# A graph network on one core: the sort's second layer as exact bfloat16 products, one group later, and shorter stretches between the stages

## The chip, the core and the metric

One core of a Trainium2 chip runs the whole program in one launch. The metric is the device time of that launch in microseconds; the time before is the median of three runs, 7716.12 us (7713.63 to 7728.18). Below, PE is the matrix engine (TensorE), DVE is VectorE, ACT is ScalarE, POOL is GpSimd and SP the engine that queues most DMAs.

## The reference, cut to what matters

The input is a table x of 6250 nodes x 64 features and 200,000 edges (src, dst, 24 attributes, a weight). Four graph layers follow each other, each with a residual and a layer norm:

```python
x = _layernorm(x + L0(x, edge_attr_8, edge_attr_16, edge_weight, ..., src, dst))
x = _layernorm(x + L1(x, edge_index, edge_weight))   # 3 proximal smoothing steps
x = _layernorm(x + L2(x, edge_index, W1, b1, W2, b2)) # polynomial of degree 5
x = _layernorm(x + L3(x, edge_index, W1, b1, W2, b2)) # two graph convolutions
# in L0, for each edge, with two small perceptrons over its attributes:
_mlp2 = lambda x, W1, b1, W2, b2: silu(x @ W1 + b1) @ W2 + b2
# their two results are added, weighted by the edge's cutoff and used in the message
# in L3:
h = x @ W; agg = segment_sum(h[src] * (dinv[src]*dinv[dst])[:, None], dst)
return agg + h * (1.0 / deg)[:, None] + b
```

The two perceptrons of an edge are computed as one: 24 attributes to 128 hidden values (8 to 64 and 16 to 64), a silu, and 128 to 64. All of this is float32 in the reference.

## The kernel before

The nodes are held as 50 blocks (`NB`) of 125 lanes (`NL`), so that a table of all nodes is 125 x 3200 float32. The stages run one after the other, each in a block of its own, with every engine meeting at its end: `front` (q, k, v projections), `sort_edges`, `build_graph`, `spill_messages`, a layer norm, three calls of `scale_of_degree`, `smooth`, a layer norm, the polynomial, a layer norm, `project` and `convolve` twice, and the last layer norm.

**The sort.** `sort_edges` writes each edge's row of 70 float32 to a place in DRAM given by its two node blocks and its rank there. It goes through 196 groups (`NG`) of 8 tiles (`G`) of 128 edges (`ST`); buffers with a number 0 or 1 change with the group. For one group:

- PE: two float32 products 24 x 512 give the hidden values (L403, named `ps_h`). Then, for each of the 8 tiles, one product reads the running count of edges per block pair (L410, `ps_r`) and one adds the tile to that count (L414, `ps_c`); ACT copies the new count from PSUM (L382) before the next L410 may run. From the fifth tile on, each tile is followed by two tiles of the second layer (L424, `ps_m`, float32, `hidden` as the stationary operand and `w2` as the moving one). In the second tile stand two small products (L431, L433, `ps_f`) that number the edges of the group before which found their place full; they wait for DVE's `flagged`.
- ACT: the silu of both hidden halves (L379) and the eight count copies.
- DVE: `group_hots` of a group (L455 to L464: the one-hot rows `hot_d`, `hot_s` over 50 blocks for its edges, and `hot_dt`, the same one-hot transposed, 50 x 1024 bfloat16), then `places` of the group before it (L483 to L511): eight comparisons of keys, the rank, the message rows (`biased` = second layer + bias at L497, times the weight at L499, the other six columns at L500), then, behind a wait for L433, the row number `row_at` of each edge (L502 to L511). Most of these are linked, that is, each waits for the one before by a semaphore.
- POOL: eight indirect stores (L351) of 128 rows each, started by `rows_ready`, which L511 counts up.
- SP: loads the attributes and keys two groups ahead.

**Between the stages.** `spill_messages` (L994 to L1074) handles the edges that found no place: 125 at a time, it loads rows, gathers q and k, v by index, sums the messages of equal targets with a product and adds them to DRAM; here it runs twice. It starts by setting a 125 x 3366 buffer to zero on POOL and writing it out. `smooth` starts with five passes of DVE over the whole table (L1782 to L1786): scale x, split it in three bfloat16 parts whose sum is exact. `posted` is then counted up for all 25 pairs of blocks at once, and PE starts. The polynomial and the convolutions start the same way (L2045, `to_parts` L1162 to L1165). Before each convolution `project` multiplies all 50 blocks by a 64 x 64 matrix, with PE, ACT and DVE taking two blocks at a time (L561 to L587).

## Time and profile before

| | |
|---|---|
| median of three runs | 7716.12 us |
| time of the profiled execution | 7703.81 us |
| its span | 7702.0 us |
| mean granted clock of PE | 0.964 |
| PE, DVE, ACT, POOL busy, share of the span | 88%, 76%, 56%, 32% |
| first to last store of the sort's loop | 265.50 to 2579.86 us |

One execution was profiled. The engines' busy shares are averages over stages which have different limits, so a stage's own rows have to be read: what each engine does in that stretch, and what ended its waits. A PE clock of 1.00 is 2.4 GHz, 0.50 is 1.2 GHz. Durations of matrix products overlap, as the products are pipelined: the distance between two starts is the time one takes on the engine, and the duration shown is longer. In the rows of a wait, the engine after the arrow is the one whose instruction came last.

### The profile page before, as it was taken

The page shows a single profiled execution, that of the slowest core. Times are in us where ns is not written, and L with a number is a line of the kernel's source. Part 1 is how long each engine was busy: PE and PEld are TensorE (multiplying, and loading weights), DVE is VectorE, ACT ScalarE, POOL GpSimd, SP SyncE. Part 2 cuts the span into 40 slices and gives each one's busy share as a digit, 9 for nine tenths or more (in the row PEclk, how much of TensorE's full clock was granted, in tenths as well). Part 3 has the DMA queues.
Part 4 walks back from the last instruction along what each step waited for, and adds up shares of the span by engine and source line. Part 5 has one row for each costly group of instructions (what it writes and reads, how often), then busy time and mean ns, then how long its engine had stood idle before and what let it go on. Part 6 is the DMA issues. An engine that isn't in the chain of part 4 may idle for free. (4 is left out here: it accounts for less than half of the span.)

```text
span 7702.0 us, 278354 instructions
## 1 busy us (share of the span) xinstructions
PE 6739.4 (88%) x98572; PEld 5729.8 (74%) x98572; DVE 5845.4 (76%) x17002; ACT 4337.5 (56%) x13124; POOL 2472.2 (32%) x2927
## 2 busy tenths in 40 slices
PE   2699999999999899999993898898995999998888
PEld 1455555555555699999993898897995999997878
DVE  4577777777777799898995899898897776765556
ACT  0122222222222599999993787887894666665545
POOL 0466666666666555454552000000000000000000
PEclk9999999999999999999996999999997999998979
DMA  9522222222222477666774888888894677763645
GB/s 392 181 64 64 63 63 64 64 63 62 65 64 63 138 232 233 225 229 227 231 233 155 296 322 296 305 323 288 324 344 155 203 201 203 201 197 111 196 134 157
DMA packets 629164, 1430.29 MB, mean 186 GB/s; under 512 B 248466, under 2 KB 281049, under 8 KB 624927
## 3 DMA queue, kind: packets, MB, share of 16 engines
q1 hardware_dynamic: 542480, 1234.12, 50.3%
q0 software_dynamic: 71904, 92.78, 4.2%
q10 hardware_dynamic: 14232, 96.26, 3.3%
q8 instruction: 322, 5.28, 0.3%
q14 instruction: 226, 1.85, 0.1%
HBM read 989.29 MB, written 436.68 MB: 185 GB/s over the span
## 5 line engine op out<-in xcount | busy, mean ns | idle before, releaser
L351 POOL DMA_INDIRECT sorted_rows<-sort_rows,sort_row_at x1568 | 1589.2, 1013 | 813.3 <-issue 536.0
L1637 ACT ACTIVATE smooth_msg<-smooth_ps_a,smooth_w_rows 128x64 f32<-128x64 f32 x6000 | 1308.3, 332 | 266.1 <-PE smooth_ps_a L1727 249.9
L382 ACT ACTIVATE sort_count<-sort_ps_c 50x50 bf16<-50x50 f32 x1568 | 323.1, 206 | 1807.1 <-PE sort_ps_c L414 1716.8
L1412 ACT ACTIVATE poly_cast<-poly_mat 128x1536 bf16<-128x1536 uint8 x500 | 714.8, 1475 | 441.9 <-PE poly_ps L1433 367.5
L424 PE MATMUL sort_ps_m<-sort_w,sort_hidden 128*128 128x64 f32 x3136 | 876.8, 434 | 0.0
L403 PE MATMUL sort_ps_h<-sort_attrs,sort_w 24*128 24x512 f32 x784 | 812.0, 1137 | 36.7 <-DMA sort_attrs<-in_attr_t 36.7
L1749 PE MATMUL smooth_ps_s<-smooth_msg,smooth_hot 128*128 128x64 bf16 x7500 | 771.0, 194 | 71.0 <-DVE smooth_last_part L1877 48.8
L410 PEld LDWEIGHTS sort_ps_r<-sort_count,sort_hot_dt 50*128 50x128 bf16 x1568 | 157.5, 100 | 869.7 <-issue 602.9
L1749 PE MATMUL smooth_ps_s<-smooth_rest,smooth_hot 128*128 128x64 bf16 x7500 | 766.5, 194 | 14.0 <-issue 14.0
L1749 PE MATMUL smooth_ps_s<-smooth_last_part,smooth_hot 128*128 128x64 bf16 x7500 | 765.7, 194 | 11.9 <-issue 11.9
L424 PEld LDWEIGHTS sort_ps_m<-sort_w,sort_hidden 128*128 128x128 f32 x3136 | 729.4, 324 | 40.3
L1749 PEld LDWEIGHTS smooth_ps_s<-smooth_msg,smooth_hot 128*128 128x128 bf16 x7500 | 687.6, 99 | 78.5 <-DVE smooth_last_part L1877 64.7
L763 ACT ACTIVATE graph_hot_t<-graph_ps_t 128x1024 bf16<-128x1024 bf16 x625 | 641.0, 1026 | 116.1 <-PE graph_ps_t L806 85.2
L1749 PEld LDWEIGHTS smooth_ps_s<-smooth_rest,smooth_hot 128*128 128x128 bf16 x7500 | 690.3, 99 | 19.8 <-issue 19.8
L1749 PEld LDWEIGHTS smooth_ps_s<-smooth_last_part,smooth_hot 128*128 128x128 bf16 x7500 | 686.9, 98 | 18.3 <-issue 18.3
L839 PE MATMUL graph_ps_kv<-kv_whole,graph_hot_t 125*128 125x128 bf16 x7500 | 685.9, 219 | 0.0
L1433 PE MATMUL poly_ps<-parts,poly_cast 125*128 125x192 bf16 x7500 | 639.4, 249 | 48.5 <-DVE poly_cast L1496 23.8
L1433 PEld LDWEIGHTS poly_ps<-parts,poly_cast 125*128 125x128 bf16 x7500 | 630.4, 99 | 57.1 <-issue 27.5
L1867 DVE TENSOR_TENSOR smooth_rest<-smooth_msg 128x640 f32<-128x640 f32 x750 | 615.9, 821 | 51.6 <-ACT smooth_msg L1637 34.9
L836 PE MATMUL graph_ps_q<-q_whole,graph_hot_t 125*128 (+1 forms) x7500 | 633.4, 193 | 15.1 <-ACT graph_hot_t L763 10.6
L1877 DVE TENSOR_TENSOR smooth_last_part<-smooth_rest 128x640 bf16<-128x640 f32 x750 | 614.8, 820 | 24.1 <-DVE sums_rest L1841 2.8
L733 POOL TENSOR_TENSOR graph_parts<-graph_parts 128x260 f32<-128x260 f32 x625 | 387.4, 620 | 744.6 <-DVE graph_hot L895 730.8
(342 smaller groups left out, 16117.7 us busy)
## 6 DMA issues: line engine op xcount, KB each, us to landing
poly_mat<-counts_t SPq DMA_DIRECT2D x500, 400.0 KB, 3.6
smooth_src<-src_rows SPq DMA_DIRECT2D x150, 960.0 KB, 5.0
smooth_hot<-hot_rows SPq DMA_DIRECT2D x150, 960.0 KB, 7.1
smooth_src<-src_rows SPq DMA_DIRECT2D x150, 640.0 KB, 6.1
smooth_hot<-hot_rows SPq DMA_DIRECT2D x150, 640.0 KB, 7.3
graph_edges<-sorted_rows SPq DMA_DIRECT2D x125, 700.0 KB
hot_rows<-graph_hot SPq DMA_DIRECT2D x125, 640.0 KB, 3.5
src_rows<-graph_hot_t SPq DMA_DIRECT2D x125, 640.0 KB, 3.4
```

Source lines behind the costliest of these rows:

```text
L351: pool.indirect_dma_start(out=sorted_rows, out_offset=bass.IndirectOffsetOnAxis(row_at[u][:, j:j + 1], 0), in_=rows[u][:, j, :], in_offset ...
L403: nc.tensor.matmul(ps_h[h][:, 0:H * ST], w1[:], attrs[u][:, h * H * ST:(h + 1) * H * ST], start=True, stop=True).then_inc(hidden_ps, 1)
L424: last = nc.tensor.matmul(ps_m[u][0:ST, t * D:(t + 1) * D], hidden[u][:, t * ST:(t + 1) * ST], w2[:], start=True, stop=True, skip_group_ch ...
L763: act.activation(hot_t[x.b][:, :, :, x.s, :].rearrange("p e t v d -> p e t (v d)"), ps_t[x.g % 2][:].rearrange("p e t v d -> p e t (v d)") ...
L836: nc.tensor.matmul(ps_q[:, 2 * t + v], d_t, q[:, i], start=i == 0, stop=i == 2, skip_group_check=True)
L839: last = nc.tensor.matmul(ps_kv[u][:, 2 * t + v], s_t, kv_parts[:, s, i], start=i == 0, stop=i == 2, skip_group_check=True)
L1412: act.activation(cast[u][h][:, DVE_S:HR, :], mat[u][h][:, DVE_S:HR, :], ACT.Copy)\
L1433: last = nc.tensor.matmul(ps[u][:, 0:3 * D], cast[u][b // HR][0:NL, b % HR, :], parts[k % 2][:, b].rearrange("p i d -> p (i d)"), start=b ...
L1637: last = act.activation(at[:, i, :], ps_a[g % 2][:, i * D:(i + 1) * D], ACT.Copy, scale=w_rows[u][:, c * CHUNK + i:c * CHUNK + i + 1])
L1749: last = nc.tensor.matmul(ps_s[u][:, 0:D], hot[u][t][:, at // 2, :, at % 2], part[:, i, :], start=False, stop=c == N_CHUNKS - 1 and i == C ...
L1867: dve.tensor_tensor(rest[c][:], msg[c][:], high(msg[c]), ALU.subtract).then_inc(firsts, 1)
L1877: dve.tensor_tensor(last_part[c][:], rest[c][:], high(rest[c]), ALU.subtract)\
```

## The change

**In the sort.** The second layer of a group is computed while PE works on the next group. DVE splits the hidden values (128 x 1024 float32) exactly: the upper 16 bits of each float32, read in place with a step of two bfloat16 (`high`), are the first part; `hidden_rest` is what is left, its upper half the second part, and `hidden_last` the third. `w2` and the bias are split in three parts once, before the loop. PE then adds nine bfloat16 products per tile, and one product of 128 x 512 for the bias. DVE multiplies the result by the edge's weight straight from PSUM (`products`, L555), which replaces L497 and L499. `rows_ready` is now counted up by `products`, so POOL's stores of a group start one group later. The one-hot `hot_dt` is made by ACT in two steps for the next group: |block - lane| and then max(0, 1 - that). DVE makes `hot_d` and `hot_s` two groups ahead. SP also writes the zeros that the spill stage needs, at the end of the sort.

**Between the stages.** `spill_messages` takes two tiles of 125 in one pass (`n_pairs` passes instead of `n_spilled`) and no longer writes zeros. The three calls of `scale_of_degree` become one block. The split of the table before `smooth` and the polynomial is done in five pieces of ten blocks, each posted by itself (`first_parts`); in the polynomial the pieces stand between casts of the first matrices. `project` and the convolution's split become `conv_rows`: PE transposes four blocks at a time straight from x, multiplies eight blocks into one PSUM bank, DVE scales from there, and ACT and DVE make the three parts of eight blocks at a time. `convolve` posts all pairs at once.

The order of PE's instructions in the sort's loop, before, for one even group from its third tile on (register instructions left out; `ps_r`, `ps_c`, `ps_m` as above, the number at a name is its buffer):

```order
L410 MATMUL sort_ps_r0<-sort_count1,sort_hot_dt0 128x50
L414 MATMUL sort_ps_c<-sort_hot_s0,sort_hot_d0 50x50
L410 MATMUL sort_ps_r0<-sort_count0,sort_hot_dt0 128x50
L414 MATMUL sort_ps_c<-sort_hot_s0,sort_hot_d0 50x50
L424 MATMUL sort_ps_m0<-sort_w2,sort_hidden0 128x64 x2
L410 MATMUL sort_ps_r0<-sort_count1,sort_hot_dt0 128x50
L414 MATMUL sort_ps_c<-sort_hot_s0,sort_hot_d0 50x50
L424 MATMUL sort_ps_m0<-sort_w2,sort_hidden0 128x64 x2
L410 MATMUL sort_ps_r0<-sort_count0,sort_hot_dt0 128x50
L414 MATMUL sort_ps_c<-sort_hot_s0,sort_hot_d0 50x50
```

The second layer of the group's own hidden values (`hidden0`) stood behind its fifth tile. The same place after:

```order
L452 MATMUL sort_ps_r0<-sort_count1,sort_hot_dt0 128x50
L456 MATMUL sort_ps_c<-sort_hot_s0,sort_hot_d0 50x50
L452 MATMUL sort_ps_r0<-sort_count0,sort_hot_dt0 128x50
L456 MATMUL sort_ps_c<-sort_hot_s0,sort_hot_d0 50x50
L471 MATMUL sort_ps_m1<-sort_b2_rows,sort_ones 128x512
L477 MATMUL sort_ps_m1<-sort_w2_parts,sort_hidden1 128x64 x3
L477 MATMUL sort_ps_m1<-sort_w2_parts,sort_hidden_rest 128x64 x3
L477 MATMUL sort_ps_m1<-sort_w2_parts,sort_hidden_last 128x64 x3
L477 MATMUL sort_ps_m1<-sort_w2_parts,sort_hidden1 128x64 x3
L477 MATMUL sort_ps_m1<-sort_w2_parts,sort_hidden_rest 128x64 x3
L477 MATMUL sort_ps_m1<-sort_w2_parts,sort_hidden_last 128x64 x3
L452 MATMUL sort_ps_r0<-sort_count1,sort_hot_dt0 128x50
```

Behind the fifth tile now stand the bias product and eighteen bfloat16 products with the other group's hidden values (`hidden1`), and eighteen behind each later tile.

DVE in the sort's loop before, for one odd group from the rank to the row numbers:

```order
L492 TENSOR_TENSOR sort_rank<-sort_rank_in,sort_base 128x8
L493 TENSOR_SCALAR sort_spills<-sort_rank 128x8
L494 SCALAR_TENSOR_TENSOR sort_slot_row<-sort_rank,sort_grp1 128x8
L497 TENSOR_TENSOR sort_biased<-sort_ps_m1,sort_b2 128x512
L499 TENSOR_TENSOR sort_rows1<-sort_biased,sort_grp1 128x8x64
L500 COPY sort_rows1<-sort_grp1 128x8x6
L502 COPY sort_spill_ps<-sort_ps_f 128x16
L503 SCALAR_TENSOR_TENSOR sort_upto<-sort_one_cols,sort_so_far,sort_spill_ps 128x8
```

Here the two 128 x 512 passes stood behind the rank. After, for one odd group from its comparisons on:

```order
L569 SCALAR_TENSOR_TENSOR sort_same,sort_rank_in<-sort_key_row1,sort_grp1,sort_before 128x128 x8
L555 TENSOR_TENSOR sort_rows0<-sort_ps_m0,sort_rows0 128x8x64
L577 TENSOR_TENSOR sort_picked<-sort_ps_r1,sort_hot_s1 128x400
L579 TENSOR_REDUCE sort_base<-sort_picked 128x8
L580 TENSOR_TENSOR sort_rank<-sort_rank_in,sort_base 128x8
L581 TENSOR_SCALAR sort_spills<-sort_rank 128x8
L582 SCALAR_TENSOR_TENSOR sort_slot_row<-sort_rank,sort_grp1 128x8
L584 TENSOR_TENSOR sort_hidden_rest<-sort_hidden1 128x1024
L585 TENSOR_TENSOR sort_hidden_last<-sort_hidden_rest 128x1024
L587 COPY sort_rows1<-sort_grp1 128x8x6
```

The multiplication of the group before (`rows0`) moved ahead of `picked`, and the two 128 x 1024 passes took the place of `biased` and `rows`.

ACT in the sort's loop after, for one group from its fourth tile on:

```order
L416 ACTIVATE sort_count1<-sort_ps_c 50x50
L394 ACTIVATE sort_lane_gap<-sort_block_row0,sort_less_lane 50x1024
L416 ACTIVATE sort_count0<-sort_ps_c 50x50
L399 ACTIVATE sort_hot_dt0<-sort_lane_gap,sort_one_cols 50x1024
L416 ACTIVATE sort_count1<-sort_ps_c 50x50
```

The two passes over 50 x 1024 are for the group that follows (`hot_dt0` while the count copies are of the odd group), ahead of the sixth and the seventh count copy.

The diff, cut to its core:

```diff
+                def turned_hots(g, u, part):
+                    if part == 0:
+                        act.wait_ge(loaded[u], g * 32 + (64 - 32 * u))
+                        act.activation(lane_gap[:], block_row[u][:], ACT.Abs, bias=less_lane[0:NB, 0:1]).then_inc(gaps, 1)
+                    else:
+                        act.wait_ge(gaps, g + 1)
+                        if not isinstance(g, int) or g >= 2:
+                            act.wait_ge(based, g - 1)
+                        act.activation(hot_dt[u][:], lane_gap[:], ACT.Relu, scale=-1.0, bias=one_cols[0:NB, 0:1])\
+                           .then_inc(hots_t, 1)
...
+                        if j in (5, 6) and not last:
+                            turned_hots(n + 1, 1 - u, j - 5)
...
-                        if j == H:
-                            pe.wait_ge(silu, 2 * n + 2)
-                        if j >= H:
-                            for t in (2 * (j - H), 2 * (j - H) + 1):
-                                last = nc.tensor.matmul(ps_m[u][0:ST, t * D:(t + 1) * D],
-                                                        hidden[u][:, t * ST:(t + 1) * ST], w2[:], start=True,
-                                                        stop=True, skip_group_check=True)
-                    last.then_inc(mixed, 1)
+                        if j >= H and first != 0:
+                            mixes(n - 1, 1 - u, first, j - H)
...
+                def mixes(m, u, first, quarter):
+                    if quarter == 0:
+                        pe.wait_ge(halved, m + 1)
+                        if first is None:
+                            pe.wait_ge(rows_ready, m - 1)
+                        nc.tensor.matmul(ps_m[u][0:ST, :], ones[0:3, :], b2_rows[0:3].rearrange("p g d -> p (g d)"),
+                                         start=True, stop=True, skip_group_check=True)
+                    for t in (2 * quarter, 2 * quarter + 1):
+                        edges = slice(t * ST, (t + 1) * ST)
+                        for part in (high(hidden[u]), high(hidden_rest), hidden_last[:]):
+                            for i in range(3):
+                                last = nc.tensor.matmul(ps_m[u][0:ST, t * D:(t + 1) * D], part[:, edges], w2_parts[:, i, :],
+                                                        start=False, stop=True, skip_group_check=True)
+                    if quarter == G // 2 - 1:
+                        last.then_inc(mixed, 1)
...
+                def group_hots(g, u):
+                    if not isinstance(g, int) or g >= 2:
+                        dve.wait_ge(counted, g * G - G)
...
-                    dve.tensor_scalar(hot_dt[u][:], block_row[u][:], lane_col[0:NB, 0:1], None,
...
+                def products(m, u):
+                    dve.wait_ge(mixed, m + 1)
+                    dve.tensor_tensor(rows[u][:, :, 0:D], ps_m[u][0:ST, :].rearrange("p (g d) -> p g d", g=G),
+                                      rows[u][:, :, W:W + 1].to_broadcast([ST, G, D]), ALU.mult).then_inc(rows_ready, 1)
...
+                    if not isinstance(g, int) or g >= 1:
+                        products(g - 1, 1 - u)
...
-                    dve.wait_ge(mixed, g + 1)
+                    dve.wait_ge(silu, 2 * g + 2)
+                    nxt(dve.tensor_tensor(hidden_rest[:], hidden[u][:], high(hidden[u]), ALU.subtract))
+                    dve.tensor_tensor(hidden_last[:], hidden_rest[:], high(hidden_rest), ALU.subtract).then_inc(halved, 1)
                     dve.wait_ge(stored[u], 16 * G * it)
-                    nxt(dve.tensor_tensor(biased[:], ps_m[u][0:ST, :].rearrange("p (g d) -> p g d", g=G),
-                                          b2[:, 2:3, :].to_broadcast([ST, G, D]), ALU.add))
-                    dve.tensor_tensor(rows[u][:, :, 0:D], biased[:], grp[u][:, :, 2:3].to_broadcast([ST, G, D]), ALU.mult)
-                    dve.tensor_copy(rows[u][:, :, D:ROW], grp[u][:, :, 0:6])
+                    nxt(dve.tensor_copy(rows[u][:, :, D:ROW], grp[u][:, :, 0:6]))
                     dve.wait_ge(prefixed, g + 1)
...
-                    dve.tensor_tensor(row_at[u][:], spill_row[:], slot_row[:], ALU.add).then_inc(rows_ready, 1)
+                    nxt(dve.tensor_tensor(row_at[u][:], spill_row[:], slot_row[:], ALU.add))
+                    if with_hots:
+                        group_hots(g + 2, u)
...
+                    sp.dma_start(edges[:], sorted_rows[bass.ds(N_SLOTS + t * (2 * TE), 2 * TE), :]
+                                 .rearrange("(i p) c -> p i c", i=2)).then_inc(got, 16)
...
+                    for i in two:
+                        for e, of in ((0, of_dst), (1, of_src)):
+                            pool.indirect_dma_start(out=of[:, i, :], out_offset=None, in_=qkv_rows,
+                                                    in_offset=bass.IndirectOffsetOnAxis(from_at[:, i, e:e + 1], 0))\
+                                .then_inc(fetched, 16)
...
+def first_parts(link, dve, posted, parts, xs, x, scale, rest):
+    for b in range(0, NB, FIRST):
+        at = slice(b, b + FIRST)
+        link(dve.tensor_tensor(xs[:, at], x[:, at], scale[:, at].unsqueeze(2).to_broadcast([NL, FIRST, D]), ALU.mult))
+        link(dve.tensor_copy(parts[:, at, 0, :], xs[:, at]))
+        link(dve.tensor_tensor(rest[:, at], xs[:, at], parts[:, at, 0, :], ALU.subtract))
+        link(dve.tensor_copy(parts[:, at, 1, :], rest[:, at]))
+        dve.tensor_tensor(parts[:, at, 2, :], rest[:, at], parts[:, at, 1, :], ALU.subtract).then_inc(posted, FIRST // 2)
...
+                def scale(o):
+                    dve.wait_ge(product, o + 1)
+                    s = octs[o]
+                    dve.tensor_tensor(xs[:, s, :], ps_o[o % 2][0:NL, 0:size(s) * D].rearrange("p (b d) -> p b d", d=D),
+                                      dinv[:, s].unsqueeze(2).to_broadcast([NL, size(s), D]), ALU.mult).then_inc(scaled, 1)
+                def rest(o):
+                    dve.wait_ge(firsts, o + 1)
+                    dve.tensor_tensor(left[:, octs[o], :], xs[:, octs[o], :], parts[:, octs[o], 0, :], ALU.subtract)\
+                       .then_inc(rests, 1)
...
+        def before_vector(dve, link, posted):
+            dve.sem_inc(posted, NB // 2)
+            return
+            yield
```

## Rows read from the trace of the kernel before

**Rows 1.** The page, busy time: engine, us, share of the span, instructions.

```profile
PE 6739.4 (88%) x98572; PEld 5729.8 (74%) x98572; DVE 5845.4 (76%) x17002; ACT 4337.5 (56%) x13124; POOL 2472.2 (32%) x2927
```

**Rows 2.** Busy us (and instructions) by stretch: window, length, engines, granted clock, DMA share, GB/s.

```profile
265.50:2560.60 2295.10, 2148.70 (x7353) 1273.58 (x7353) 1648.54 (x7379) 535.76 (x1937) 1573.50 (x1553) 1.00 0.27 63
```

**Rows 3.** Waits from 240 to 2560 us: engine, line, released by, us, times, longest us.

```profile
DVE sort_spill_ps L502 <- PE sort_ps_f L433: 458.6, 187, 2.6
...
POOL sorted_rows L351 <- DVE sort_row_at L511: 275.3, 178, 1.7
```

**Rows 4.** PE in the timeline: start us, duration us, engine, line, operation, count, [idle before].

```profile
2541.46 2.07 PE L403 MATMUL sort_ps_h<-sort_attrs,sort_w 24*128 24x512 f32 x2
...
2548.16 1.12 PE L424 MATMUL sort_ps_m<-sort_w,sort_hidden 128*128 128x64 f32 x4
...
2549.21 0.22 PE L410 MATMUL sort_ps_r<-sort_count,sort_hot_dt 50*128 50x50 bf16 x1
...
2553.31 2.07 PE L403 MATMUL sort_ps_h<-sort_attrs,sort_w 24*128 24x512 f32 x2
```

**Rows 5.** DVE in the timeline, one group of the sort.

```profile
2546.36 0.17 DVE L502 COPY sort_spill_ps<-sort_ps_f 128x16 f32<-128x16 f32 x1 [2.33 <-PE sort_ps_f L433]
...
2552.27 0.57 DVE L489 TENSOR_TENSOR sort_picked<-sort_ps_r,sort_hot_s 128x400 f32<-128x400 f32 x1
...
2554.05 0.69 DVE L497 TENSOR_TENSOR sort_biased<-sort_ps_m,sort_b 128x512 f32<-128x512 f32 x1
...
2554.78 0.69 DVE L499 TENSOR_TENSOR sort_rows<-sort_biased,sort_grp 128x512 f32<-128x512 f32 x1
...
2555.39 0.18 DVE L500 COPY sort_rows<-sort_grp 128x48 f32<-128x48 f32 x1
```

**Rows 6.** Lines by form: line, engine, operation, count, busy us, mean ns, idle before.

```profile
L464 DVE TENSOR_SCALAR sort_hot_dt<-sort_block_row,sort_lane_col 50x1024 bf16<-50x1024 bf16 x196 | 110.7, 565 | 0.0
...
L1867 DVE TENSOR_TENSOR smooth_rest<-smooth_msg 128x640 f32<-128x640 f32 x750 | 615.9, 821 | 51.6 <-ACT smooth_msg L1637 34.9 <-DVE smooth_norm L1813 4.1 <-DVE smooth_shrink L1824 0.8
...
L763 ACT ACTIVATE graph_hot_t<-graph_ps_t 128x1024 bf16<-128x1024 bf16 x625 | 641.0, 1026 | 116.1 <-PE graph_ps_t L806 85.2
...
L351 POOL DMA_INDIRECT sorted_rows<-sort_rows,sort_row_at x1568 | 1589.2, 1013 | 813.3 <-issue 536.0 <-DVE sort_row_at L511 277.0 <-DVE sort_pad_at L527 0.3
```

**Rows 7.** POOL in the timeline, a store with nothing in its way.

```profile
2542.53 0.97 POOL L351 DMA_INDIRECT sorted_rows<-sort_rows,sort_row_at  x1 [0.30 <-issue]
```

**Rows 8.** PE in the timeline, smoothing: first and last of 30 products.

```profile
5500.56 0.20 PE L1749 MATMUL smooth_ps_s<-smooth_msg,smooth_hot 128*128 128x64 bf16 x1 [0.21 <-DVE smooth_last_part L1877]
...
5501.43 0.19 PE L1749 MATMUL smooth_ps_s<-smooth_last_part,smooth_hot 128*128 128x64 bf16 x1
```

**Rows 9.** SP and POOL queues in the timeline, spill stage.

```profile
4090.14 21.00 SPq L1005 DMA_DIRECT2D spill_edges<-sorted_rows  x2
...
4086.01 2.90 POOL L1014 MEMSET spill_zeros<- 125x3366 f32 x1 [4.14 <-ACTq L994]
...
4106.42 2.03 POOL L1025 DMA_INDIRECT y_rows<-spill_total,spill_to  x1 [5.67 <-DVE spill_total L1074]
...
4122.39 2.03 POOL L1025 DMA_INDIRECT y_rows<-spill_total,spill_to  x1 [5.69 <-DVE spill_total L1074]
```

**Rows 10.** DVE in the timeline, before the smoothing's first products.

```profile
4179.67 3.49 DVE L1782 TENSOR_TENSOR xs<-x,dinv 125x3200 f32<-125x3200 f32 x1 [9.83 <-DMA smooth_lane_col<-in_lanes]
...
4194.08 0.19 DVE L1788 TENSOR_SCALAR smooth_less_scale<-dinv 125x50 f32<-125x50 f32 x1
```

**Rows 11.** Busy time by stretch, the first projection.

```profile
7081.00:7128.00 47.00, 41.45 (x150) 27.48 (x150) 11.23 (x50) 22.98 (x100) 0.00 (x0) 0.50 0.00 0
```

**Rows 12.** DVE, then PE in the timeline, before the first convolution's products.

```profile
7131.02 3.49 DVE L2045 TENSOR_TENSOR xs<-node_sums,dinv 125x3200 f32<-125x3200 f32 x1 [3.66 <-DMA conv_lane_col<-in_lanes]
...
7145.43 3.83 DVE L1496 CAST conv_cast<-conv_mat 128x1664 bf16<-128x1664 uint8 x4
...
7146.56 10.86 PE L1433 MATMUL conv_ps<-parts,conv_cast 125*128 125x192 bf16 x98 [19.59 <-DVE conv_cast L1496]
```

More of the change, by code:

```diff
@@ L441, in _ @@
                 prefixes(NG)
+                for quarter in range(G // 2):
+                    mixes(NG - 1, (NG - 1) % 2, None, quarter)
             @blk.vector
@@ L446, in _, with link @@
                 dve.wait_ge(made, 2)
[L447 to L456 removed]
+                def link(ins, value):
+                    ins.then_inc(step, 1)
+                    dve.wait_ge(step, value)
@@ L1042, in _ @@
-                dve.wait_ge(const, 64)
+                n = count(dve)
+                STEPS = 9
+                dve.wait_ge(const, 32)
                 with dve.Fori(0, n) as t:
```

412 lines of the change are left out of this document (236 added, 176 removed).

## The prediction

> **What bounds the kernel now.** I read the page's busy times first [rows 1]: PE is busy for 88% of the span. That is a mean over ten stages, so next came the busy time by stretch. The sort's loop [rows 2] is 2295 us of 7702, at a granted clock of 1.00, with PE busy for 2149, DVE for 1649, POOL for 1574 and ACT for 536. The chain of waits is of no use here: its followed part covers the last layer norm alone. The waits of the sort [rows 3] say which engine is late: DVE stood still 187 times at L502 for PE's L433, 458.6 us, 2.45 us each, and POOL stood still for DVE's L511, 275.3 us. So the order is PE, then DVE, then POOL, each behind the other. The timeline gives the period: PE's group starts at 2541.46 and the next at 2553.31 [rows 4], 11.85 us. There are 193 steady periods among the 196 groups. So PE bounds the sort, DVE has 2.45 us of slack per group and its own work is 11.85 - 2.45 = 9.40.
>
> **PE after.** Up to the fifth tile nothing on PE changes: 2541.46 to 2548.16, 6.70 us [rows 4]. Then stand four quarters of 2548.16 + 1.05 = 2549.21 for the float32 second layer and 0.315 for the next tile's two products; 3 x 1.365 + 1.05 = 5.15 ends the group. The new quarter is 18 bfloat16 products of 64 columns. Thirty such products, their weights from the same kind of view (a step of two), started from 5500.56 to 5501.43 [rows 8], 0.030 us each. So a quarter is 0.54 instead of 1.05. With 0.2 for the bias product, PE's own group is 6.70 + 0.2 + 4 x 0.54 + 3 x 0.315 = 10.0 us. ACT's two new passes stand between count copies that PE waits for. Each has 1024 elements a lane, and L763 with 1024 took 1.03 us [rows 6]; PE has 0.54 of products between two counts to cover it, so up to 0.5 us may be lost at each of two places. The nearest bounds for PE are 10.0 and 11.0; I take 10.4.
>
> **DVE after.** Gone: L464 on DVE, 0.57 us busy, some 0.50 of it not overlapped [rows 6]; L497, from 2554.05 to 2554.78, 0.73 [rows 5]. L499 (0.61 to 2555.39) is replaced by `products`, the same size, read from PSUM as L497 was: no change. New: two passes of 128 x 1024, two inputs, one with a step of two. L1867 is that operation on 640 elements, 821 ns [rows 6], and 512 elements take 0.69 [rows 5]: 1.02 ns an element, so 1.21 us busy, and with a link 1.26, without 1.15; together 2.4. Nearest bounds: 1.1 if each ran like the 1024 of L464, 2.9 if the link and start cost 0.25 each. Four more waits and one more link: 0.3, from the 0.05 to 0.1 by which linked starts lie further apart than unlinked ones. The sum is 9.40 - 0.50 - 0.73 + 2.4 + 0.3 = 10.9 us. The wait for L433 falls away, since DVE now arrives there after it. `hot_d` and `hot_s` two groups ahead cost nothing by themselves.
>
> **POOL after.** L351 took 1589.2 us for 1568, and 536.0 us of issue with them, of which 87 are one wait at the start: (1589.2 + 449)/196 = 10.4 us a group [rows 6]. It fits below 10.9. Its start now hangs on `products`, one group later, which delays it but doesn't lengthen its period; DVE's wait for its stores (`stored`) is for those of two groups before. The last of them starts 0.6 + 7 x 1.3 = 9.7 us after `products` began, and the wait comes 10.9 + 0.6 + 1.8 + 2.4 = 15.7 after, which leaves 6 us for its landing.
>
> **The round.** `picked`, its sum and the rank took 1.8 us, from 2552.27 to 2554.05 [rows 5]. The split needs the silu, the products need the split, `products` needs them, and the next split stands behind `products`, `picked` and the rank: 4 x 0.54 + 3 x 0.315 + 0.2 + 0.3 + 0.6 + 1.8 + 2.4 = 8.4 us, below 10.9. PE's wait for `halved` at its fifth tile is 6.7 us after its group starts, and DVE's split ends some 5 us after `mixed`: no wait. So DVE is the bound, at 10.9, and PE idles about 0.5 us a group.
>
> The sort: (11.85 - 10.9) x 193 = **-183 us**. Ends of the loop: the last group's stores come one turn of products later, +4; and some of the first groups' work lies before the stores may begin at all (265.50), -3: together +1, with bounds of -5 and +12 (a whole group).
>
> **The stages between.** Spill: the second pass, from 4106.42 to 4122.39, goes, -16.0 [rows 9]; two more gathers and one more store with its landing lengthen the first by 3 + 4. The zeros went, POOL's L1014 of 2.90 us from 4086.01 with the load behind it at 4090.14, and that load was queued behind the writing of zeros: -6. Sum -15. What SP writes instead lies behind the sort's last groups, where SP has nothing to do. Degrees: three blocks in one, two of the meetings of the engines less, -2. Smooth: five passes took 14.4 us from 4179.67 to 4194.08 [rows 10]; in pieces there are 25 instead of 5, 20 more at 0.15: +3, and the pieces that PE can start on early win nothing, since DVE must be through before it can take PE's first results. If they did, up to -10. The polynomial: about -0.5, as its pieces stand between casts. Each `project`: PE was busy for 41.45 of 47 us [rows 11], and its waits of two blocks at a time for ACT go; the clock was 0.50 there and I keep it: -4. Each convolution: DVE's 14.4 us of passes from 7131.02 to 7145.43 go from before the first cast, and PE began at 7146.56 [rows 12]; next late is the load of the first matrix and its cast, about 2 us after DVE could begin: -12.3. Two of each: 2 x -16.3 = -33.
>
> **Sum.** -183 + 1 - 15 - 2 + 3 - 0.5 - 33 = -229.5. Against the profiled execution, 7703.8, that is 7474. This one lay 12.3 us below the median, so against the median of 7716.1 it is **7486 us**.
>
> **The shared port.** Of DVE and POOL the rows show this: a store L351 took 0.97 us undisturbed [rows 7] and 1013 ns in the mean [rows 6], 0.04 more each and 0.35 us a group, while DVE has about 3.8 us of passes with two inputs in each group. The Trainium skill, "SBUF — State Buffer", section "Terms", calls the port pair that DVE and GpSimd share an exclusive lock which lets the loser block fully; the two new passes both have two inputs in SBUF. By that rule POOL could lose up to their whole length; by the row it loses a tenth of what DVE spends. The trace so far does not agree with a full block of every store.
>
> **Rivals.**
> (a) PE stays the bound. For it: weights read with a step of two load slower than the smoothing's rows show, or ACT's passes cost their full 0.5 twice and more. At 0.054 for twelve and 0.030 for six of each quarter, a quarter is 0.83 and PE 11.2 us with ACT's delays small: (11.85 - 11.2) x 193 = -125, 7544 us. Against it: [rows 8] have the same step. Chance 0.10.
> (b) DVE's passes are cheaper or better overlapped (2 us instead of 2.4, waits free) and the period is PE's or POOL's 10.4: -280 + rest -46.5, 7390 us; in it too are the convolutions' products at the upper clock. Chance 0.10.
> (c) Slower: POOL is blocked for the length of both new passes. Place: L351 beside L584 and L585. Price: 2.4 us a group on 10.4, so 12.8 us a period, +183, with the rest -46.5: 7853 us. It decides from the point at which POOL loses over 1.7 us a group (10.4 + 1.7 against the 12.1 that cancels the other gains). For it: POOL works all through the group now, so it can't evade. Against it: a loss of 0.35 beside 3.8 us of such passes. Chance 0.04.
> (d) Slower: PE, now waiting in each group and with smaller products, gets the lower clock in the sort: its 4.0 us of hidden-layer products and 2.2 of quarters twice would make the period 10.0 + 6.2, some 16 us, and the time 8450 to 8500. For it: convolution and projection stretches at 0.50 [rows 11]. Against it: 1.00 through the loop [rows 2] with PE busy for 94% of it, which falls only to some 90%. Chance 0.03.
> (e) The gain in the sort is nothing because the round of silu, split, products and POOL closes at 11.8: only the other stages remain, -46.5, 7670 us. Against it: 8.4 us for the round. Chance 0.04, of it 0.01 within the bound.
>
> **Numbers.** The forecast of 7486 has 0.69. Its own range follows from 10.5 to 11.2 us a period and 10 us on the rest, 7400 to 7560, and that holds (a) and (b) in part, and leaves 2 in 10 outside. A difference of over 0.2%, 15 us, can be told in this kernel. Faster: 0.69 + 0.10 + 0.10 + 0.03 = 0.92; within 0.01; slower 0.04 + 0.03 = 0.07.
>
> **What would show it.** In the changed kernel: the sort's group at 10.9 us between two equal starts of DVE, with no wait at L589 and waits of PE on DVE or ACT instead; L584 and L585 at 1.2 us each; products of L477 0.030 us apart; L351 at a mean of 1.02 us or so; the granted clock at 1.00 in the loop. A mean of L351 over 1.2 us would speak for (c), L477 more than 0.04 apart for (a). The spill stage should be 15 us shorter, the first convolution's first product 12 us earlier after its block begins. The prediction is wrong if the period is under 10.5 or over 11.2.

## The result, and the profile after

The changed kernel takes 7701.81 us (median of 20 runs, 7688.45 to 7714.97) against 7715.95 for the one before (20 runs): a ratio of 0.998, 95% interval 0.9973 to 0.9987. It is faster by 14 us, where 230 were forecast. A second measurement gave 7686.72 against 7710.79, 0.9968 (0.9954 to 0.9983).

The profiled execution has a span of 7698.7 us. The page's busy times and its row of the granted clock, each digit one fortieth of the span, answer to [rows 1]:

```profile
PE 6743.7 (88%) x109744; PEld 5759.3 (75%) x109744; DVE 6071.1 (79%) x16972; ACT 4745.7 (62%) x13370; POOL 2605.9 (34%) x2927
...
PEclk9755555555555799999997999999997999998889
```

The clock stands at 0.5 in the slices of the sort. Busy time of the loop, as in [rows 2]:

```profile
265.50:2584.00 2318.50, 2151.89 (x18470) 1290.28 (x18470) 1882.51 (x7368) 952.63 (x2331) 1707.07 (x1551) 0.54 0.25 63
```

PE is busy as before, at 0.54. The waits of the loop, as in [rows 3]:

```profile
PEld sort_ps_r L452 <- ACT sort_count L416: 279.7, 625, 34.7
...
DVE sort_rows L555 <- PE sort_ps_m L477: 254.7, 139, 37.1
...
POOL sorted_rows L371 <- DVE sort_rows L555: 108.1, 82, 1.7
```

DVE still waits for PE, now at L555 for the nine products: 254.7 us where it was 458.6. PE and DVE in one group and a half, as in [rows 4, 5]:

```profile
1510.05 2.07 PE L444 MATMUL sort_ps_h<-sort_attrs,sort_w 24*128 24x512 f32 x2
...
1516.75 0.60 PE L471 MATMUL sort_ps_m<-sort_b_rows,sort_ones 3*128 3x512 bf16 x1
...
1517.28 0.34 PE L477 MATMUL sort_ps_m<-sort_w_parts,sort_hidden 128*128 128x64 bf16 x3
...
1517.43 0.35 PE L477 MATMUL sort_ps_m<-sort_w_parts,sort_hidden_rest 128*128 128x64 bf16 x3
...
1518.07 0.35 PE L477 MATMUL sort_ps_m<-sort_w_parts,sort_hidden_last 128*128 128x64 bf16 x3
...
1518.35 0.22 PE L452 MATMUL sort_ps_r<-sort_count,sort_hot_dt 50*128 50x50 bf16 x1
...
1519.75 0.22 PE L452 MATMUL sort_ps_r<-sort_count,sort_hot_dt 50*128 50x50 bf16 x1
...
1521.84 1.12 PE L444 MATMUL sort_ps_h<-sort_attrs,sort_w 24*128 24x512 f32 x2
...
1510.15 0.69 DVE L555 TENSOR_TENSOR sort_rows<-sort_ps_m,sort_rows 128x512 f32<-128x512 f32 x1 [2.00 <-PE sort_ps_m L477]
...
1512.55 1.23 DVE L584 TENSOR_TENSOR sort_hidden_rest<-sort_hidden 128x1024 f32<-128x1024 f32 x1
...
1513.81 1.23 DVE L585 TENSOR_TENSOR sort_hidden_last<-sort_hidden_rest 128x1024 bf16<-128x1024 f32 x1
```

The six rows of three products in a quarter start from 1517.28 to 1518.07, 0.158 us apart, so a product takes 0.053 us and not 0.030. A quarter is 1518.35 - 1517.28 = 1.07 us, and the step from one quarter to the next 1.40.
```profile
L351 POOL DMA_INDIRECT sorted_rows<-sort_rows,sort_row_at x1568: 969/972/1412, 265.5 to 2579.9; - x196
```

(columns: minimum, median and maximum in ns, first and last start), and after:

```profile
L371 POOL DMA_INDIRECT sorted_rows<-sort_rows,sort_row_at x1568: 971/975/1998, 273.7 to 2604.9; - x196
```

The ledger by the first instruction of each stage in the two profiled executions: the sort with its end +25.0 us, the graph's building +1.6, the spill stage -13.0, the degrees and what lies before them -3.0, the smoothing +4.9, the polynomial +0.9, the first projection -6.8, the first convolution with the second projection -9.3, the rest -3.5. The sum is -3.3 (each rounded); without the sort -28.3. In the profile of the second measurement the sort ends 13.1 us later than before, so its loss is known only as 13 to 25 us.

Why the two convolutions gave so little shows in the waits of the first, before and after (240 us from the stage's start):

```profile
DVE conv_cast L1496 <- DMA conv_mat<-counts: 4.3, 1, 4.3
...
ACT conv_cast L1412 <- DMA conv_mat<-counts: 12.6, 3, 6.8
```

```profile
DVE conv_cast L1554 <- DMA conv_mat<-counts: 23.4, 9, 6.1
...
ACT conv_cast L1472 <- DMA conv_mat<-counts: 21.0, 8, 6.2
...
7143.91 10.82 PE L1493 MATMUL conv_ps<-parts,conv_cast 125*128 125x192 bf16 x98 [10.75 <-ACT conv_cast L1472]
```

The first block is of before, the second of after. PE begins 5.9 us after the stage does, where it was 18.0: the 12 us forecast. But the 14.4 us of DVE's passes had also covered the loading of the matrices, and now DVE waits for them nine times and ACT eight, 23.4 and 21.0 us.

### The profile page after: what moved, and what is told of

Same layout as the page of the kernel before. It is cut to its first block and busy times, and to the rows that moved or that the text cites. A ratio compares the mean times of both kernels' runs of the same rounds, so it can differ in the third digit from the quotient of the medians.

```text
span 7698.7 us, 301254 instructions
## 1 busy us (share of the span) xinstructions
PE 6743.7 (88%) x109744; PEld 5759.3 (75%) x109744; DVE 6071.1 (79%) x16972; ACT 4745.7 (62%) x13370; POOL 2605.9 (34%) x2927
## 5 line engine op out<-in xcount | busy, mean ns | idle before, releaser
L371 POOL DMA_INDIRECT sorted_rows<-sort_rows,sort_row_at x1568 | 1723.7, 1099 | 703.9 <-issue 594.3
L1811 PE MATMUL smooth_ps_s<-smooth_last_part,smooth_hot 128*128 128x64 bf16 x7500 | 770.0, 194 | 15.6 <-issue 15.5
L444 PE MATMUL sort_ps_h<-sort_attrs,sort_w 24*128 24x512 f32 x784 | 717.4, 1010 | 2.0 <-DMA sort_attrs<-in_attr_t 2.0
L1811 PEld LDWEIGHTS smooth_ps_s<-smooth_rest,smooth_hot 128*128 128x128 bf16 x7500 | 692.4, 99 | 12.4 <-issue 12.4
L1554 DVE CAST poly_cast<-poly_mat 128x1664 bf16<-128x1664 uint8 x500 | 510.5, 1031 | 60.9 <-DMA poly_mat<-counts_t 54.4
L1789 PE MATMUL smooth_ps_a<-parts,smooth_src 125*128 125x64 bf16 x12000 | 447.3, 195 | 101.9 <-DVE parts L1224 68.6
```

Source lines behind the costliest of these rows:

```text
L371: pool.indirect_dma_start(out=sorted_rows, out_offset=bass.IndirectOffsetOnAxis(row_at[u][:, j:j + 1], 0), in_=rows[u][:, j, :], in_offset ...
L444: nc.tensor.matmul(ps_h[h][:, 0:H * ST], w1[:], attrs[u][:, h * H * ST:(h + 1) * H * ST], start=True, stop=True).then_inc(hidden_ps, 1)
L1554: dve.tensor_copy(cast[u][h][:, 0:DVE_S, :], mat[u][h][:, 0:DVE_S, :]).then_inc(cast_v, 1)
L1811: last = nc.tensor.matmul(ps_s[u][:, 0:D], hot[u][t][:, at // 2, :, at % 2], part[:, i, :], start=False, stop=c == N_CHUNKS - 1 and i == C ...
```

## The experiments

Median times are set against the kernel before on the same chip. On three chips that kernel took 7707 to 7711 us. On two it took 8093 and 8184; the text calls them the slower chips. In the traces taken on them ACT stands still for up to 7 us at a time in the loop, and the mean granted clock, 0.965 to 0.968, is no lower than elsewhere.

**The stages alone.** The edit: `sort_edges` of before in the changed program, with the spill zeros written at its end.

> The sort of before with all the changes between the stages (it also writes the spill stage's zeros at its end). By the stage boundaries in the two traces the changed sort is 25 us longer and all the rest 28 us shorter. If these add up, this kernel takes 7716 - 28 = 7688 us (0.9964 of before) and is 14 us faster than the changed one. The rival, by which the stages' gain depends on the new sort, gives 7700 or more. By the forecast's sum the stages were worth 47 us: 7669.

Measured: 7672.11 us against 7706.81, 0.9956 (0.9943 to 0.997), -35 us. So the stages pay, somewhat better than the boundaries say, and the changed sort costs time: the changed kernel, at 0.998 and 0.9968 of before, is slower than this one, and the graph's building begins at 2588.7 us here and at 2613.4 there.

**Which clock the sort of before had.** The edit puts 300 bfloat16 products ahead of the loop.

```diff
+                for _ in range(300):
+                    nc.tensor.matmul(ps_f[0:ST, 128:256], ones[:], ones[:], start=True, stop=True,
+                                     skip_group_check=True)
```

> The kernel before, with 300 bfloat16 products of 128 columns on PE ahead of the sort's loop, in time that the loop waits for the zero fills anyway; nothing else changes. Theory A (the clock column shows 1.00 only because no change of the clock had been recorded yet; in truth the sort of before ran at 1.2 GHz): the products rise to the upper clock, and after them the column shows 0.50 in the loop, with the same period of 11.85 us, the same 2.07 us for a pair of L403's records and the same time, within 10 us of 7716. Theory B (the sort of before ran at 2.4 GHz, and the changed one fell from it): the column shows 1.00 in the loop and everything else is the same.

Measured: 7708.36 us against 7706.81, 1.0004 (0.9995 to 1.0013). The stretches (as in [rows 2]), and the two records of one float32 product in the loop:

```profile
215.00:240.00 25.00, 21.90 (x192) 15.47 (x189) 7.28 (x32) 6.25 (x15) 0.00 (x0) 0.77 1.01 414
...
300.00:1000.00 700.00, 655.89 (x2248) 389.32 (x2248) 501.77 (x2244) 163.26 (x591) 479.33 (x473) 0.50 0.26 63
...
1501.09 2.07 PE L406 MATMUL sort_ps_h<-sort_attrs,sort_w 24*128 24x512 f32 x2
```

Theory A. The product takes 2.07 us, as in [rows 4], the time is the same, and the column now reads 0.50 in the loop. That the burst itself lowered the clock is ruled out by the same 2.07 us and the same time. So the column reads 1.00 up to the first recorded change, whatever the clock is; in before that change comes at 2602 us, behind the sort. It reads 1.00 in the loops of the kernels with float32 products one group late and with six products below too, where L444 takes 2.07 us throughout. The trace of before had this in it. Rows of nearly equal kind stood there, four records of float32 products with 64 columns (the second with 64 rows of weights instead of 128): 1.12 us in the sort under a shown clock of 1.00 (2548.16 in [rows 4]) and 1.10 us in the projection under 0.50 [rows 11]:

```profile
7125.88 1.10 PE L579 MATMUL conv_of_ps_o<-w,conv_of_block_t 64*125 64x64 f32 x4 [0.15 <-ACT conv_of_block_t L566]
```

**Float32 products, one group late.** The edit puts one float32 product for the nine and keeps all else.

```diff
-                        for part in (high(hidden[u]), high(hidden_rest), hidden_last[:]):
-                            for i in range(3):
...
+                        last = nc.tensor.matmul(ps_m[u][0:ST, t * D:(t + 1) * D], hidden[u][:, edges], w2[:],
+                                                start=False, stop=True, skip_group_check=True)
```

> The changed kernel with the second layer as one float32 product a tile again, still one group later and with the bias product; DVE's two splitting passes stay. If the sort ran and runs at 1.2 GHz, a quarter is 1.05 us for the float32 products and 1.07 for the nine bfloat16 ones: the group is 11.85 + 0.6 for the bias product = 12.45 us, all of it at the lower clock, so 12.45 x 193 against 11.85 x 193 with the stages' -34: 7710 - 34 + 115 = 7790. The changed kernel beats it only by its short stretches at the upper clock. If the nine products had been the slow part, this kernel is at or below 7702.

> Float32 products one group late with the bias product. Where before takes 7710: 7790, a group of 12.45 us, if both second layers cost PE the same at 1.2 GHz. On the two slower chips it took 0.991 and 0.995 of before; if before is over 8000 again, the same.

Measured twice on the slower chips: 0.991 and 0.9951 of before. On a chip where before takes 7710.79: 7794.48 us against 7710.79, 1.0101 (1.0085 to 1.0118), as expected to 5 us:

```profile
1503.87 0.60 PE L471 MATMUL sort_ps_m<-sort_b_rows,sort_ones 3*128 3x512 bf16 x1
...
1504.40 1.11 PE L475 MATMUL sort_ps_m<-sort_w,sort_hidden 128*128 128x64 f32 x4
...
1505.77 1.12 PE L475 MATMUL sort_ps_m<-sort_w,sort_hidden 128*128 128x64 f32 x4
...
1509.55 2.07 PE L444 MATMUL sort_ps_h<-sort_attrs,sort_w 24*128 24x512 f32 x2
...
1521.93 2.07 PE L444 MATMUL sort_ps_h<-sort_attrs,sort_w 24*128 24x512 f32 x2
```

The step from quarter to quarter is 1.37 (1.40 with nine), the bias product 0.53, the group 12.38. So at 1.2 GHz nine bfloat16 products cost what one float32 product costs (1.07 us against some 1.05 for two tiles). Their whole gain in the changed kernel is that with them short stretches at the upper clock occur, 12.4 to 11.9 us; and the bias product took as much away, 0.53 us.

**Six of the nine products.** Second times third, third times second and third times third are left out, below 2 to the minus 24 of the result.

```diff
-                        for part in (high(hidden[u]), high(hidden_rest), hidden_last[:]):
-                            for i in range(3):
+                        for k, part in enumerate((high(hidden[u]), high(hidden_rest), hidden_last[:])):
+                            for i in range(3 - k):
```

> The changed kernel without the three smallest of the nine products per tile (second times third part, third times second, third times third, below 2 to the minus 24 of the result): 12 instead of 18 products in each quarter. If PE bounds the changed sort at the lower clock (0.053 us a product), the period falls by 4 x 6 x 0.053 = 1.3 us from some 12.0 to DVE's 10.9: 1.1 x 193 = 210 us less, 7490. If DVE or POOL bounds it already, nothing changes, 7702.

> Six products a tile. Where before takes 7710: 7597 to 7605 again. Where before takes over 8000, PE is not the bound and the six products win little: within 1% of changed_again.

Measured: 7596.66 us, 0.9854 (0.9839 to 0.9869), and again 7594.75, 0.9842 (0.9826 to 0.9859). The gain over the changed kernel is 105 us where 210 were forecast. PE was the bound, but two things stood against it. With six products no stretch at the upper clock occurs in the loop, so PE's own group is 12.49 - 24 x 0.053 = 11.22 us (the shortest groups take 11.21), not DVE's 10.9. And POOL stopped the rest, as the group took 11.43 us in the mean:

```profile
L371 POOL DMA_INDIRECT sorted_rows<-sort_rows,sort_row_at x1568 | 1733.4, 1105 | 601.2 <-issue 600.9 <-DVE sort_pad_at L617 0.3
...
DVE sort_rows L587 <- DMA sorted_rows<-sort_rows,sort_row_at: 158.2, 160, 2.1
```

POOL stood still for nothing but its issues: 8 x (1.106 + 0.325) = 11.45 us a group, and DVE waited 160 times for the landing of its stores. I had given POOL 10.4. The mean store was 1105 ns here and 1097 in the second run of the same kernel.

**Filling PE's waits.** Five idle products at each of three places.

```diff
+                        if first is None and 2 <= j <= 4:
+                            if j == 2:
+                                pe.wait_ge(rows_ready, n - 2)
+                            for _ in range(5):
+                                nc.tensor.matmul(ps_m[1 - u][0:ST, 0:64], ones[:], ones[:, 0:64], start=True, stop=True,
+                                                 skip_group_check=True)
```

> The changed kernel with five idle bfloat16 products of 64 columns (0.27 us at the lower clock) in each of the three places where PE waits for ACT's count copy, 0.15 to 0.30 us each. If the clock follows how densely PE works, the share of the loop at the upper clock rises well over the present 0.07 and the period falls below 11.5: under 7620. If the float32 products of the first layer alone bring it down, the share stays and the time is within 20 us of 7702, or above it where the filling does not fit in the waits.

Measured: 7741.79 us, 1.0058 (1.0041 to 1.0076). From 1000 to 2000 us PE was busy for 989 us instead of 930, at a clock of 0.54, as without the filling, and the kernel was slower: 1.0058 of before, where the changed one is 0.998.

**The first layer in bfloat16.** The edit: `high(w1)` and `high(attrs[u])` as operands of L444; the lower halves are left out.

> The changed kernel with nine products a tile and the first layer as one bfloat16 product of the upper halves (the rest of the attributes and weights is left out): 0.43 us at the lower clock, 0.21 at the upper, instead of 2.0. If the float32 products are what brings the clock down in each group, the upper clock holds in most of the loop (over 0.8 on average) and POOL bounds the period at about 11.2: 7560. If the waits for ACT bring it down, the clock stays near 0.55 and PE's group is 12.4 - 3.1 = 9.3 us at the lower clock, and the period is again POOL's 11.2: the same time, another clock.

Measured: 7583.98 us (one run; its group by the stores 11.33).

```profile
1000.00:2000.00 1000.00, 752.13 (x8222) 526.47 (x8222) 854.64 (x3354) 436.30 (x1059) 768.80 (x708) 0.56 0.25 66
```

The clock stayed at 0.56, though no float32 product was left in the loop, and POOL set the time. The edit changes two things at once, as PE is also less busy without them, 75% instead of 93%. So filling the waits alone did not hold the clock up, nor did taking out the float32 products alone; both together were not tried, and what would hold it up in this loop stays open.

**What holds POOL's stores.** Three kernels. With three products and no hidden_last:

```diff
-                    nxt(dve.tensor_tensor(hidden_rest[:], hidden[u][:], high(hidden[u]), ALU.subtract))
-                    dve.tensor_tensor(hidden_last[:], hidden_rest[:], high(hidden_rest), ALU.subtract).then_inc(halved, 1)
+                    dve.tensor_tensor(hidden_rest[:], hidden[u][:], high(hidden[u]), ALU.subtract).then_inc(halved, 1)
```

> The changed kernel with three products a tile (first times first and second part, second times first) and without the pass that makes hidden_last; parts below 2 to the minus 16 of the result are left out. The kernel with six products had a period of 11.2 us, POOL without a gap at 8 x (1.105 + 0.3) us, and DVE waiting for POOL's stores. If POOL is the bound there and what stretches its stores from 0.97 to 1.1 us is DVE's passes beside them, the mean of L371 falls to about 1.04 us and the period to 10.7: about 7500. If PE was the bound, it falls by 4 x 6 x 0.053 + 0 = 1.3 us: 7350. If POOL's time does not depend on DVE, it stays at 11.2: 7597.

Measured: 7599.02 us against 7709.76, 0.9858 (0.9841 to 0.9875), L371 at a mean of 1086 ns. PE's work fell by another 1.3 us a group and DVE's by one pass, and nothing came of it: POOL was the bound. The forecast of 1.04 us for a store was wrong. With hidden_last made from one input (`tensor_scalar` by 0.0, which leaves out the third part):

> Six products a tile, and hidden_last made by a pass of the same size with one tensor input (the second part of the values is wrong by it). If a store is held up by DVE's passes with two tensor inputs in SBUF, the mean of L371 falls from 1.105 us to about 1.05. If it is held up by any busy DVE, it stays, or falls only as the pass gets shorter.

Measured: 7607.23 us (one run), L371 1094 ns, which is within what two runs of the kernel with six products differ by (1097 and 1105). That pass, 0.69 us instead of 1.23, frees almost nothing. Without both passes:

> The changed kernel without DVE's two splitting passes, and with three products a tile, of the first part of the hidden values alone (the rest is left out). It shows what POOL's stores cost without those passes. The mean of L371 was 1013 ns before, 1099 in the changed kernel, 1105 with six products and 1086 with one of the two passes. If the passes hold the stores up, it is about 1030 here and the period, which POOL sets, 8 x (1.03 + 0.325) = 10.85 us. If POOL is held up by something else, it stays at 1080 and 11.3.

> Without DVE's two passes, three products of the first part alone. The mean of L371 was 993 ns in the first run of it, against 1086 to 1105 with one or both passes. If POOL is the bound with six products, its period here is 8 x (0.993 + 0.325) = 10.5 us, or PE's 4.1 + 2.5 + 0.1 + 1.05 + 0.54 + 4 x 0.32 = 9.6 us and what ACT's two passes of 1.14 us hold up, 1 us: about 10.6. The time is then 7716 - 34 - 1.3 x 193 = 7430.

Both runs fell on slower chips (8360.22 and 8300.71 us), so of their times nothing follows, and whether the period would be 10.6 was not measured. The stores' own durations were 993 and 992 ns, longest 1336 in the second. POOL waited 988 and 934 us for L556 there, so the stores also stood at other places of the group.

**The passes in pieces.**

```diff
+                    for q in range(4):
+                        a = slice(q * 256, (q + 1) * 256)
+                        last = dve.tensor_tensor(hidden_rest[:, a], hidden[u][:, a], high(hidden[u])[:, a], ALU.subtract)
+                    nxt(last)
```

(and the same for `hidden_last`; six products)

> Six products a tile, and each of DVE's two splitting passes as four of 256 columns. Single stores of 1.95 us stand beside these passes, so a store seems to wait until the pass is over. If it waits for one instruction only, the pieces shorten it: the mean of L371 falls from 1.106 to about 1.06 and the period from 11.45 to 11.1, 7597 - 65 = 7530. If it waits until DVE pauses, nothing is won: 7597, or more by DVE's six extra starts.

> Six products and DVE's passes in pieces of 256 columns. Where before takes 7710: 7577, if DVE's added starts make it the bound at 11.35 us, or 7530 if POOL alone counts (8 x 1.384 = 11.1). On the slower chips it took 1.029 and 1.021 of before.

Measured twice on the slower chips: 1.0287 and 1.0214 of before. On a chip where before takes 7710.79: 7569.84 us against 7710.79, 0.9813 (0.9796 to 0.9829), the fastest of all:

```profile
L371 POOL DMA_INDIRECT sorted_rows<-sort_rows,sort_row_at x1568: 969/983/1392, 272.6 to 2467.3; - x196
...
L371 POOL DMA_INDIRECT sorted_rows<-sort_rows,sort_row_at x1568 | 1648.8, 1052 | 640.7 <-issue 636.7 <-DVE sort_rows L555 4.0
...
DVE sort_rows L593 <- DMA sorted_rows<-sort_rows,sort_row_at: 31.6, 66, 1.4
...
1500.11 0.60 PE L471 MATMUL sort_ps_m<-sort_b_rows,sort_ones 3*128 3x512 bf16 x1
...
1511.31 0.60 PE L471 MATMUL sort_ps_m<-sort_b_rows,sort_ones 3*128 3x512 bf16 x1
...
1504.72 0.69 DVE L555 TENSOR_TENSOR sort_rows<-sort_ps_m,sort_rows 128x512 f32<-128x512 f32 x1 [0.20 <-PE sort_ps_m L477]
...
1515.92 0.69 DVE L555 TENSOR_TENSOR sort_rows<-sort_ps_m,sort_rows 128x512 f32<-128x512 f32 x1 [0.29 <-PE sort_ps_m L477]
```

The mean store is 1052 ns, the longest 1392 instead of 1959, and DVE's wait for the stores is down from 151 us to 32. PE and DVE both go round in 11.20 us, which is PE's own group with six products at the lower clock (11.22 above): PE is the bound again.

**The smoothing's split in one piece** (with six products).

> Six products a tile, and the split of the table before the smoothing in one piece of 50 blocks, as before, instead of five. By the stage boundaries the smoothing became 4.9 us longer with the pieces; without them it is 3 to 5 us shorter, so 7593 us beside 7597. If the pieces had no part in it, the stage stays 4.9 us longer than before; read from the boundaries, as the time alone does not tell 4 us.

Measured: 7608.85 us against 7709.76, 0.9865 (0.9848 to 0.9881). The stage took 1708.4 us by its boundaries, with pieces 1709.4 in the kernel with six products, 1711.9 in the one with the stages alone and 1700.6 in the changed one. It varies by more than the 5 us in question: inconclusive. By the same boundaries it took 1695.7 us in the kernel before and 1699.8 in the one with the burst, and 1698 to 1715 in all kernels with the changed stages, this one without pieces among them. What lengthens it there was not found.

**The changed kernel beside the last three.**

> The changed kernel itself beside the kernel before, in the same call as the next three, because on the two chips of the last calls the kernel before took 8093 and 8184 us instead of 7710. Where before takes about 7710 this one takes 7702. Where it takes over 8000 (ACT standing still for its instructions in each turn of the loop), this one's ACT has two passes more in the chain of count copies, and it is slower than before, by 1% or more.

Measured: 7686.72 us, 0.9968, on a chip where before takes 7710.79; what it does on the slower ones was not measured.

## Why the prediction was wrong

**PE after: the step that failed.** It read thirty products of the smoothing as "0.030 us each. So a quarter is 0.54 instead of 1.05", and took the clock of the sort from the 1.00 of [rows 2]. The products were 0.053 apart, the quarter 1.07, the bias product 0.53 and not 0.2; PE's group at the lower clock 12.49 us and not 10.0 to 11.0. The sort did not win 183 us but lost 25 (13 in the second profile). Shown: by the burst, which made the column read 0.50 with nothing else changed, and by the float32 products one group late, 7794.48 where this account gave 7790. The rate was the right one for smoothing and the wrong one for this stage. Rival (a), PE stays the bound, came true with its own sign, L477 more than 0.04 us apart, but for another reason: it blamed the step of two, for twelve of the eighteen products, and gave 7544. Rival (d) named the lower clock, but as a fall from the upper one, priced at 8450 to 8500 (its own 10.0 + 6.2 us gives 8510), and missed that the 11.85 us of before already contained it. That (e), with its 7670, lies nearest in number is luck, as its round of 11.8 us was not what closed.

**DVE after: the passes right, the sum 0.5 us too high.** Each new pass is busy for 1.225 us against 1.21, with 1.26 and 1.14 from start to start against 1.26 and 1.15. DVE's own group, its round less its waits for the other engines and for the stores, is 11.90 - 1.56 = 10.3 us in the changed kernel (276 us of such waits in 176 groups) and 11.43 - 1.10 = 10.3 with six products (193 us in 175), not 10.9. Which of the smaller terms was too high was not separated; it cost nothing, as DVE was not the bound in any of these runs.

**POOL after: mis-sized.** 10.4 us forecast, 11.45 measured where it is the bound (six products). Two parts: the stores were assumed to stay at 1013 ns, and were 1106; the issue between two was 0.325. Even with PE at the upper clock, POOL would have held the period: (11.85 - 11.45) x 193 = 77 us of gain in the sort instead of 183. That is an estimate from these rows, for no run had PE at the upper clock.

**The shared port: partly right against me.** Single stores beside DVE's splitting passes took up to 2.0 us, where the longest before was 1.41. The first row is of the changed kernel, beside L584 at 1512.55 above, the others of the one with six products:

```profile
1513.00 1.62 POOL L371 DMA_INDIRECT sorted_rows<-sort_rows,sort_row_at  x1 [0.30 <-issue]
...
1507.50 1.95 POOL L371 DMA_INDIRECT sorted_rows<-sort_rows,sort_row_at  x1 [0.30 <-issue]
...
1507.38 1.23 DVE L584 TENSOR_TENSOR sort_hidden_rest<-sort_hidden 128x1024 f32<-128x1024 f32 x1
...
1508.64 1.23 DVE L585 TENSOR_TENSOR sort_hidden_last<-sort_hidden_rest 128x1024 bf16<-128x1024 f32 x1
```

The store at 1507.50 began 0.12 us behind DVE's first pass and lost 0.98 of that pass's 1.23 us; the one at 1513.00 began 0.45 us behind it and lost 0.65. In both, the loss is what was left of the pass when the store began, less 0.13 us. This holds for all 194 stores that began within L584 in the kernel with six products, to 0.03 us, and they hold 157 of the 205 us that its stores lost. None of them lost anything to L585 behind it, and the 188 that began within L585 did so in its last 0.12 us and lost nothing, so the two kernels that leave L585 out or shorten it could show little. The mean rose by 0.086 us a store, 0.7 a group, not by the 2.4 of rival (c): of the eight stores of a group about one falls within L584. By the Trainium skill, "SBUF — State Buffer", section "Terms", the lock is held for the full instruction; the trace agrees with it in that the loss lasts to the end of the pass, and in that beside passes of a quarter of the length no store took over 1.24 us (the longest, 1.39, stood beside another pass, L548). That the loss depends on two inputs is not shown: in the kernel with the one-input pass no store began within that pass.

**The round, the ends.** No wait of PE for `halved` was forecast; it came to 15.6 us in all from 240 to 2400. DVE's wait for the stores, which I had given 6 us of room, came to 48 us in the changed kernel and to 151 and 158 with six products.

**The stages.** Forecast -47.5 (the -46.5 of the rivals has the +1 of the sort's ends in it), measured -35 (0.9956) in the kernel with these alone. Spill -13 against -15 and degrees -3 against -2: right. The projection gave -6.8 against -4. For the smoothing, +4.9 against +3, its variation of up to 19 us lets nothing be said. The convolutions: PE did begin 12 us sooner, and 3 to 4 us of each were left. The step named "the load of the first matrix" as next late; late were the loads behind it, nine waits of DVE and eight of ACT.

## What to carry to other kernels

Before a duration from one stage is used in another, compare two rows of one and the same form in both: equal durations under different shown clocks mean that the column is blind in one of them, as it is up to the first change on record. When a bound is to be lifted by 20%, price every other engine as it will run then, with no gaps and beside the new instructions, for here POOL stood 3% behind. Work that is taken away from ahead of a stage also takes its cover from the loads that ran beneath it.

## What was not expected of the hardware

With nine bfloat16 products a tile PE goes to the upper clock for a few microseconds in some groups: from 300 to 2400 us 44 times, each time within the eighteen-product quarters, and it falls back within the first-layer products. With six products or one float32 product a tile it never did so in the loop. With its waits filled (busy for 98.9%) it rose 47 times, and fell back also within the filling (17 times); without any float32 product it rose 78 times and fell back all the same. It is not the gaps alone nor the float32 products alone.

On two of the five chips of the experiments, the same kernel before took 8093 and 8184 us, 5 to 6% more, and the kernel with pieces, which is 1.9% faster elsewhere, was 2.1 and 2.9% slower there. In its traces ACT's waits in the loop that no other engine or DMA explains came to 545 and 632 us of 2000. That a chain through ACT's count copies costs more where ACT halts would fit this; no run tests it.
